# Two small attentions rebuilt with unrolled loops, and in the recurrence the corner blocks moved to ScalarE

## The reference

```python
for i in range(H):                       # L0_attn, H = 16
    q_rot, k_rot = rotary(q[:, i], freq_i), rotary(k[:, i], freq_i)
    att = einsum('btd,bsd->bts', q_rot, k_rot) * scale
    if cascade_bias is not None:
        att = att + cascade_w[i - 1] * cascade_bias
    att = softmax(causal(att))           # next head's bias comes from att
...
for t in range(T):                       # L1_attn, per sequence and head, S and R are 64 x 64
    kn = k / max(norm(k), 1e-12)
    r = clip(v - S.T @ kn, -1, 1)
    S = a * S;   S = S + b * outer(kn, v - S.T @ kn)
    R = aR * R;  R = R + g * outer(kn, r - R.T @ kn)
    o = S.T @ q + R.T @ q
...
q = lora(x, Wq, bq, Aq, Bq)              # L3_xattn, 16 heads, keys and values from the context
k, v = split(lora(feature, Wf, bf, Af, Bf))
out = lora(softmax(causal(q @ k.T / sqrt(8))) @ v, Wp, bp, Ap, Bp)
```

## Time and profile before

| | us |
|---|---|
| median of 3 runs | 3740.51 (3736.25 to 3745.74) |
| the profiled execution | 3746.5 |
| its span, first to last instruction | 3744.7 |
| l0_attn, first product to last add | 170.4 to 461.2 |
| l1_attn, first load to the next sublayer's | 1121.9 to 2421.7 |
| l3_xattn, first product to the block's end | 3414.7 to 3542.0 |
| mean granted TensorE clock (1 is 2.4 GHz) | 0.833 |

### The profile page before, as it was taken

One profiled execution on the slowest core, in us unless ns is written; L12 is line 12 of the kernel. 1 busy time (PEld: TensorE's weight loads), 2 busy tenths in 40 slices (PEclk: granted clock), 3 DMA queues, 4 the chain that ended last, 5 costly groups with the idle time before them and its releaser, 6 DMA issues. The chain is left out here.

```text
span 3744.7 us, 117402 instructions
## 1 busy us (share of the span) xinstructions
PE 2824.1 (75%) x50001; PEld 1980.9 (53%) x50009; DVE 2288.9 (61%) x5777; ACT 1433.9 (38%) x3268; POOL 606.6 (16%) x623
## 2 busy tenths in 40 slices
PE   8852347899995687878787877759998998696654
PEld 5510136444444566666666666536665665384443
DVE  3466532556546887778877887247776555564451
ACT  4312123334333343444444443426665333363220
POOL 0040032455540000000000000000000322061014
PEclk9865567899996698989988998959998998796575
DMA  2100023111101000000000000000001001251013
GB/s 81 40 0 0 0 95 111 55 37 44 43 20 44 3 4 3 4 3 4 4 4 3 4 4 4 3 10 24 24 24 42 0 0 29 71 121 44 5 35 96
DMA packets 69034, 107.01 MB, mean 29 GB/s; under 512 B 10384, under 2 KB 55072, under 8 KB 68032
## 3 DMA queue, kind: packets, MB, share of 16 engines
q1 hardware_dynamic: 56912, 78.25, 6.8%
q0 software_dynamic: 11696, 22.40, 2.4%
HBM read 87.97 MB, written 16.51 MB: 28 GB/s over the span
## 5 line engine op out<-in xcount | busy, mean ns | idle before, releaser
L2885 PE MATMUL psum<-l1d_rw,l1d_cols 64*32 64x32 f32 (+2 forms) x20480 | 246.0, 221 | 115.0 <-issue 71.2
L2394 POOL TENSOR_TENSOR l2x_qx<-l2x_q,consts 128x128 f32<-128x128 f32 x64 | 25.5, 398 | 1723.2 <-DVE l2x_q L2565 1399.5
L2885 PEld LDWEIGHTS psum<-l1d_rw,l1d_cols 64*32 64x32 f32 x20480 | 215.9, 110 | 160.8 <-issue 109.6
L2319 POOL TENSOR_SCALAR l1xs_p<-l1xs_p,l1xs_col 128x257 f32<-128x257 f32 x256 | 238.1, 932 | 243.3 <-DVE l1xs_col L2282 242.7
L2247 ACT ACTIVATE l1xs_p<-psum,l1xs_col 128x257 f32<-128x257 f32 x256 | 122.2, 477 | 256.1 <-DVE l1xs_col L2277 255.9
L2682 ACT COPY l1d_ya<-psum 128x512 f32<-128x512 f32 x160 | 94.2, 589 | 264.4 <-PE psum L2924 264.4
L2277 DVE TENSOR_REDUCE l1xs_col<-psum 128x1 f32<-128x257 f32 x256 | 107.3, 419 | 138.5 <-PE psum L2199 138.5
L3119 DVE TENSOR_TENSOR l1d_rw<-l1d_rw,l1d_tots 128x512 f32<-128x512 f32 x240 | 152.5, 685 | 26.7 <-PE psum L2885 24.9
L2199 PE MATMUL psum<-l1xs_keys,l1xs_qx 128*32 128x257 f32 x2048 | 161.8, 396 | 3.7 <-ACT l1xs_p L2247 3.7
L2211 PE MATMUL psum<-l1xs_pt,l1xs_vals 32*128 32x512 f32 x1152 | 162.0, 637 | 1.3 <-DVE l1xs_pt L2289 1.3
L2824 PE MATMUL psum<-l1d_src,l1d_wp 128*128 128x128 f32 x1024 | 144.2, 300 | 23.3 <-ACT l1d_src L2687 23.3
(11 more groups left out here) (562 smaller groups left out, 7121.1 us busy)
## 6 DMA issues: line engine op xcount, KB each, us to landing
l2f_w<-in_l2f_w SPq DMA_DIRECT2D x16, 768.0 KB, 4.7
l1xs_vals<-in_ctx_strips SPq DMA_DIRECT2D x16, 576.0 KB, 3.8
l0x_ctxT<-in_ctxT SPq DMA_DIRECT2D x16, 516.0 KB, 3.7
l1xs_keys<-in_ctxT SPq DMA_DIRECT2D x16, 516.0 KB, 3.5
l2x_ctxT<-in_ctxT SPq DMA_DIRECT2D x64, 129.0 KB, 2.1
l1d_wp<-in_l1d_wp SPq DMA_DIRECT2D x1, 2048.0 KB, 8.0
l2f_acc<-l2f_zero SPq DMA_DIRECT2D x8, 256.0 KB, 4.5
l2f_sums<-l2f_acc SPq DMA_DIRECT2D x8, 256.0 KB, 5.1
```

Source lines behind the costliest of these rows:

```text
L2319: nc.gpsimd.tensor_scalar(p[:, t % 4, :S2], p[:, t % 4, :S2], col[:, 2, t % 4:t % 4 + 1], None, ALU.mult).then_inc(s["norm"], 1)
L2885: mm = nc.tensor.matmul(k.ps[bank0 + pr + e // per * 2][b * T:b * T + T, e % per * w:(e % per + 1) * w], cols[rr, n, e * 128 + b * T:e * 1 ...
```

## The change

It rewrites `l0_attn` as one unrolled block and drops `small_scores` and `small_values`. Scores are made as in `l3_xattn`; the head loop works on two halves of 256 columns by turns, transposes go to PE with a copy on ACT, values are laid out per head (`vd`) so that a product gives the own head's rows, and the output projection is spread over the heads with widened weights (1 MB in place of 64 KB). In `l3_xattn` values and attention are multiplied per unit (one chunk and head group) with 128 rows of weights, 64 products per chunk in place of 256, and the projection out takes 16 products of 128x128 per chunk with widened weights (1 MB more to load, and 16 more products to fold the low-rank part in). In `l1_attn` ACT copies the corner blocks out of PSUM with a column of ones and zeros as scale, PE's first fill of a tile also waits for that, `turn` negates 16 elements a row in place of 1024 and needs no memset, and each part of the inversion stands one step later in DVE's order.

```diff
# l0_attn: ahead of the head loop, on PE
+            front(0)
+            pe.wait_ge(s["set"], 2)
+            for c in range(1, NCH):
+                front(c)
+                scores(c - 1)
+            scores(NCH - 1)
+            pe.wait_ge(s["vd"], NCH)
# l0_attn: the head loop
+            def turn(h, x):
+                pe.wait_ge(s["att"], h * 2 + x + 1)
+                if h < H - 1:
+                    nc.tensor.matmul(mean_ps[x][:, :half * T], k.const("meanT"),
+                                     att[:, x, h % 2].rearrange("p n s -> p (n s)"), start=True, stop=True
+                                     ).then_inc(s["mean_mm"], 1)
+                if h * 2 + x > 0:
+                    pe.wait_ge(s["t"], h * 2 + x)
+                for j in range(2):
+                    mm = nc.tensor.transpose(t_ps[:, j * 128:(j + 1) * 128], ...)
+                mm.then_inc(s["t_mm"], 1)
+            def values(h, x):
+                pe.wait_ge(s["t"], h * 2 + x + 1)
...
+                for j in range(2):
+                    for b in range(TB):
+                        n = (2 * x + j) * TB + b
+                        mm = nc.tensor.matmul(o_ps[m, n * T:(n + 1) * T], vd[:, n, h, :], attT[:, x, j, b * T:(b + 1) * T],
+                                              start=True, stop=True)
+            for h in range(H):                      # PE
+                turn(h, 0)
+                if h > 0:
+                    values(h - 1, 1)
+                turn(h, 1)
+                values(h, 0)
+                if h >= 4:
+                    out(h // 4 - 1, h % 4)
+            def first(h, x):                        # DVE
+                src = sc[:, h, half * x:half * x + half, :]
+                if h > 0:
+                    dve.wait_ge(s["mean_mm"], (h - 1) * 2 + x + 1)
+                    step(nc.vector.scalar_tensor_tensor(a[:, x].rearrange("p n s -> p (n s)"), mean_ps[x][:, :half * T],
+                                                     cw[:, h:h + 1], src.rearrange("p n s -> p (n s)"), ALU.mult, ALU.add))
...
+                step(nc.vector.tensor_reduce(mx[:, x], src, AX.X, ALU.max))
+                nc.vector.tensor_tensor(a[:, x], src, spread(mx[:, x]), ALU.subtract).then_inc(s["shift"], 1)
+            for h in range(H):                      # DVE
+                if h > 0:
+                    second(h - 1, 1)
+                second(h, 0)
+                first(h, 1)
+                if h + 1 < H:
+                    first(h + 1, 0)
# l3_xattn: values and out
-            def values(c):
...
-                for b in range(TB):
-                    r = slice(b * T, (b + 1) * T)
-                    if b > 0:
-                        pe.wait_ge(s["own_mm"], c * TB + b)
-                    for t in range(4):
-                        for h in range(4):
-                            for g in range(4):
...
+            def values(u):
...
+                for t in range(4):
+                    for h in range(4):
+                        mm = nc.tensor.matmul(o_ps[32 * h:32 * h + 32, g * 128 + t * T:g * 128 + t * T + T],
+                                              vd[:, c % 2, t, 4 * g + h, :], attT[:, u % 2, (t * 4 + h) * T:(t * 4 + h) * T + T],
+                                              start=True, stop=True)
...
+                for b in range(TB):
+                    for g in range(4):
+                        mm = nc.tensor.matmul(out_ps[:].rearrange("p (t b q) -> p b t q", t=4, b=TB)[:, b], wp[:, g, b, :],
+                                              o[:, g, :], start=g == 0, stop=g == 3)
# l1_attn
+            def keep_l(i, n):
+
+                act.wait_ge(s[("mS", "mR")[n]], i * LEVELS + LEVELS)
+                for pr in range(2):
+                    x = k.ps[2 * n + pr][:, :(384, 256)[n]].rearrange("p (h f t) -> p h f t", h=hp, t=T // 2)
+                    ins = activation(ll[:, i % 2, n, hp * pr:hp * pr + hp, :], x[:, :, n], ACT.Identity, scale=part[:, 4:5])
+                ins.then_inc(s["ll"], 1)
...
                     take_nb(i + 1)
+                if now:
+                    keep_l(i, 0)
                 if old:
                     take(i - 2, "o_mm", rd, "B", "o")
+                if now:
+                    keep_l(i, 1)
                 if mid:
                     widen(i - 1, 1)
                     widen(i - 1, 2)
...
                 if lv == 0 and i > 0:
+                    pe.wait_ge(s["ll"], i * 2)
                     pe.wait_ge(s["mR"], i * LEVELS)
...
-                        vc.copy_predicated(ll[:, i % 2, 0, hs, :], top, part_[:, :, 0, :])
...
-                        ins = vc.copy_predicated(ll[:, i % 2, 1, hs[pr], :], top, part_[:, :, 1, :])
...
-                t(vc.tensor_scalar(xi[:, :T * T], lt[:, :T * T], -1.0, None, ALU.mult))
-                t(vc.memset(xi[:, 0:T * T:T + 1], 1.0))
+                t(vc.tensor_scalar(first(xi), first(lt), -1.0, None, ALU.mult))
...
-                if mid:
-                    merge(2)
-                if now:
                     advance_s(i, 1)
                     keep_s(i, 1)
                 if mid:
-                    merge(4)
+                    merge(2)
                 if now:
                     advance_r(i, 1)
                     keep_r(i, 1)
                 if mid:
-                    merge_last(0)
+                    merge(4)
                 if now:
                     advance_s(i, 2)
                     keep_s(i, 2)
...
                 if mid:
-                    merge_last(1)
-                    turn_back(i - 1)
+                    merge_last(0)
                 if now:
                     advance_s(i, 3)
                     keep_s(i, 3)
                     advance_r(i, 3)
                     keep_r(i, 3)
+                if mid:
+                    merge_last(1)
+                    turn_back(i - 1)
+                if now:
                     keep_s(i, 4)
```

More of the change, by code:

```diff
@@ L639, in l0_attn @@
     nc, ph = k.nc, ExitStack()
-    s = {n: k.sem("l0a_" + n) for n in ("bias_mm", "shifted", "exp", "att", "turned", "kept", "steps")}
+    s = {n: k.sem("l0a_" + n) for n in ("set", "group", "p_mm", "turn", "qk", "v_mm", "vd", "ks", "sc_mm", "kept", "step", "shift", "exp",
+                                        "att", "mean_mm", "t_mm", "t", "o_mm", "o", "out_mm", "x")}
     with ph:
         wall = k.sb("l0a_w", [128, 5, D], ctx=ph)
-        wproj = k.sb("l0a_wp", [128, D], ctx=ph)
+        wp = k.sb("l0a_wp", [128, 4, 4, D], ctx=ph)
@@ new lines, in l0_attn @@
+        half = N // 256
+        a, att = k.sb("l0a_a", [128, 2, half, T], ctx=ph), k.sb("l0a_att", [128, 2, 2, half, T], ctx=ph)
+        mx, rs = k.sb("l0a_mx", [128, 2, half], ctx=ph), k.sb("l0a_rs", [128, 2, half], ctx=ph)
+        attT, o = k.sb("l0a_attT", [128, 2, 2, 128], ctx=ph), k.sb("l0a_o", [128, 2, CH], ctx=ph)
+        mean_ps, t_ps, o_ps = k.ps[4:6], k.ps[6], k.ps[7]
+        pair = lambda c, n: 4 + 2 * ((c + n) % 2)
+        block = ph.enter_context(nc.Block())
+        @block.tensor
@@ L796, in _ @@
             pe.wait_ge(s["fold"], 1)
             front(0)
+            rows(0)
             pe.wait_ge(s["set"], 3)
-            for c in range(NCH):
-                scores(c)
-                if c + 1 < NCH:
-                    front(c + 1)
-                if c > 0:
-                    values(c - 1)
+            scores(0)
+            pe.wait_ge(s["wide"], 4)
+            scores(1)
+            for g in range(4):
+                mm = nc.tensor.matmul(o_ps[:, :1], wp[:, g, 0, :], bv[:, g:g + 1], start=g == 0, stop=g == 3)
@@ L805, in _ @@
+            mm.then_inc(s["bias_mm"], 1)
+            for u in range(units):
+                c, g = u // 4, u % 4
+                if u + 2 < units:
+                    scores(u + 2)
+                if g == 0 and c + 1 < NCH:
+                    front(c + 1)
+                if u > 0:
+                    values(u - 1)
+                if g == 1 and c + 1 < NCH:
+                    rows(c + 1)
+                if g == 2 and c > 0:
                     out(c - 1)
-            values(NCH - 1)
+            values(units - 1)
@@ L807, in _ @@
             out(NCH - 1)
-        @block.gpsimd
-        def _(pool):
-            nc.gpsimd.memset(vs[:], 0.0).then_inc(s["clear"], 1)
         @block.scalar
@@ L906, in _ @@
                                   ).then_inc(s["set"], 1)
-            last = 4 * NCH - 1
-            shift(0)
-            for u in range(last + 1):
-                if u < last:
+            for g in range(4):
+                dve.wait_ge(s["wide_mm"], g + 1)
+                x = wp[:, g].rearrange("p b d -> p (b d)")
+                nc.vector.scalar_tensor_tensor(x, k.ps[(1, 2, 3, 7)[g]][:], 1.0 / 16, x, ALU.mult, ALU.add
+                                               ).then_inc(s["wide"], 1)
+            shift(0)
+            dve.wait_ge(s["bias_mm"], 1)
+            nc.vector.tensor_tensor(cols[:, 5:6], o_ps[:, :1], bcol[:, 2:3], ALU.add).then_inc(s["bias"], 1)
```

(8 more changed lines are left out.)

575 lines of the change are left out of this document (256 added, 319 removed).

## The result

The changed kernel takes 3526.4 us (median of 4 runs, 3516.4 to 3539.7) against 3743.1 before, a ratio of 0.9425 with a 95% interval of 0.9382 to 0.9467: 217 us less, where I had forecast 165. It lies in the range, between the forecast (3575) and the rival "warm and smooth" (3518). The profiled execution took 3535.4 us, 211 less than the one of before.

What follows compares the result with a forecast made beforehand. It took waits among PE, DVE and ACT to bound l0_attn, PE l3_xattn, PE and DVE l1_attn. Gains 104 + 12 + 50 = 166 from the profiled 3746.5, less 6, gave 3575 us; range 3515 to 3632.

Steps and rivals of the forecast that it cites:

- warm and smooth: Rival (c), whole kernel: gains of 122 in l0_attn, 26 in l3_xattn, 75 in l1_attn, 223 in all, 3518 us; chance 0.13.
- l0_attn, 104 forecast: The rebuilt l0_attn block falls from 290.7 to 187 us (73 front, 102 heads, 12 rest), a gain of 104 us.
- 16 x 2.40 = 38.4: l0_attn ahead of the head loop: 16 scores groups on PE at l3_xattn's price of 2.40 us, 38.4 us.
- The head loop, 102 forecast: l0_attn's 16 heads at 6.4 us, mixing about 8.0 at half clock (6.25 without projection) and 5.65 at full: 102 us.
- l3_xattn, 12 forecast: l3_xattn on PE: values 37 us less, fold and bias 9.4 and out 12 more, 3 less for waits; gain 12.
- warm end of 28: Upper end of the l3_xattn term, with PE warm: a gain of 28 us.
- l1_attn, 50 forecast: l1_attn: clip 4.35 us earlier per pass; 48 + 12 + 2 - 3 - 9 = 50 us gained.
- 48 us: l1_attn: the part of PE step y2's 56.4 us wait for DVE's clip that was to go, 48 us.
- (a): Rival, l0_attn's head loop: PE stays at 1.2 GHz, heads take 121 us, 141 us gained, 3600 us; chance 0.22.
- (d): Rival, l0_attn: the two halves don't overlap, a head takes 17.6 us, the kernel is 14 slower, 3754 us; chance 0.03.
- (b): Rival, l1_attn: PE's queue bounds it, the wait for the clip becomes issue gaps, 128 gained, 3613 us; chance 0.14.
- Weights of 1 MB more: l0_attn and l3_xattn: wider weights load during the layer norm, costed at nothing; if late, 1 or 2 us each.

Runs made afterwards that it cites:

- e6: The changed kernel with l0_attn's output projection moved ahead of the second half's mean in the head loop; 3509.9 us, ratio 0.9366 to the kernel before.
- e7: The changed kernel with each value product in l3_xattn taking 32 of its 128 rows; 3536.0 us, l3_xattn 86.9 us.
- e8: The changed kernel with l3_xattn's fold of the wide output weights placed behind the first chunk's projections; 3531.9 us, l3_xattn 88.7 us.
- e9: The changed kernel with 12 of the 16 products of l3_xattn's projection out left out; 3536.3 us, l3_xattn 83.4 us.
- e4: The kernel before with only the new order of the merges on VectorE in l1_attn; 3694.8 us, ratio 0.9851.
- e5: The kernel before with only l1_attn's corner block copies moved to ScalarE, old merge order and full negation kept; 3742.9 us, ratio 0.9996.
- e11: The changed kernel with l1_attn's sigmoid table loaded early and the second merge, merge(4), put behind the clip; 3529.3 us, l1_attn 1217.2 us.
- e3: The kernel before with the new l1_attn alone; 3704.5 us, ratio 0.9883.
- e10: The changed kernel with l1_attn's sigmoid table loaded early, in ScalarE's idle time; 3528.4 us, l1_attn 1220.7 us.

## Why the prediction was right, and where it was not

- *l0_attn, 104 forecast, 125 measured.* The term was mis-sized in its front: "16 x 2.40 = 38.4" for the scores. Twelve of the sixteen groups took 1.33 us from start to start and only the last chunk's four took 2.40; projections and value products ran mostly at the full clock too (17.5 and 5.2 us busy, taken as 21.7 and 8). The front took 57 us to the first mean, not 73 + 2, and what follows the loop 6.5, not 10. I had carried the price of a group over from a block that ran at 0.55 of the clock.
- *The head loop, 102 forecast (6.4 a head), 101 measured.* The total is right, in part by luck. The first four heads took 5.6 us on average (I had 6.25; the first, at 0.50 of the clock, took 6.28), the ten behind them 7.0 (I had a mixture of 5.65 and 8.0 that comes to 6.4), and the last head, without a mean, is short. That the granted clock parts the quick heads from the slow ones was right: with the projection, 5.54 and 6.01 us at the full clock, 7.30 at 0.73. The step that I missed is what e6 shows: the place of the projection costs 0.86 us a head by itself and brings the lower clock with it. The unseen operation, 128 rows x 32 columns, cost 0.69 / 16 = 0.043 us at full clock, near the lower end and not the 0.08 that I took.
- *l3_xattn, 12 forecast, 38 measured, past even my warm end of 28.* Two prices were wrong in the same direction: scores (29.4 us busy before, 18.9 after, taken as unchanged) and value products (7.6 busy and 3.8 waited, taken as 17). The fold was right in itself (7.0 for 8.2), but was set against a sum of PE alone. That sum was the wrong frame. Once PE is quick, VectorE's 3.65 us per scores group bound the block; in that frame the 38 us are there, since its wait for scores fell by 28.6 us (36.7 to 8.1) and that for the projection out by 11.9 (20.0 to 8.1). A chunk takes 17.4 us (3293.61 to 3311.03, VectorE's adds to X), where I had 24 to 27. PE's values, fold and scores groups hardly count there any more (e7; e8; e9, where five of the last eight groups were slow and the block no longer for it); its projection out still does (6 us in e9).
- *l1_attn, 50 forecast, 42 to 53 measured.* The mechanism was right: what stands ahead of the clip counts, and what is put off goes into VectorE's wait at level 5 (e4), though not for nothing, since its wait ahead of `advance` grew by 32 us. From y2 to y2 a pass takes 72.0 us on average (passes with all parts at work), 75.4 before; I had 71. Inside it one size was off: "48 us" of y2's wait were to go, and 32 went (56.4 to 24.4), since the gates, 14.1 us, are late next and I had not named them. What made up for it is that the fills wait less for VectorE too, 44 us before (115.0 less 71.2 of issue) and 27 after (99.4 less 72.5). y2's own time fell by 9.3 us (51.1 to 41.8; I had 12). The copies on ScalarE cost and bring nothing, as said (e5).
- *The rivals.* (a), a head loop wholly cold, and (d), halves that do not overlap, did not come: 0.78 of the clock, 6.6 us from mean to mean (92.2 us over 14 heads). The 4 us of the earlier trace rows that spoke for (a) also hold a 128x128 mask product of 0.61 us, and are not 32x32 tiles alone. (b) did not bind here; e11 suggests that it does once y2's waits are gone. (c), "warm and smooth" at 3518, was the nearest of all cases to 3526, but by luck: its l0_attn (122) is met by a warm front and not by warm heads, its l3_xattn (26) is too low and its l1_attn (75) too high.
- *Weights of 1 MB more in two sublayers* cost little, as said: ahead of l0_attn's first product PE stands idle for 1.31 us (1.84 in the earlier trace rows), ahead of l3_xattn's for 3.02 (1.32 in the earlier trace rows).

## What to carry to other kernels

In an engine's hand-written order, ask of each piece who waits behind it: moving the corner blocks to another engine gave nothing here, while existing lines put in another place gave 42 to 51 us (the merges) and 23 us (the projection out). A price measured in a block at 0.55 of the clock is not the price of the same instruction in a rebuilt block; bound it by the same row at both levels, and ask of every engine, not only of the one that binds now, what the rebuilt block would take if that engine set the pace. When a wait has been shortened, look in the new profile at which other signal arrives within half a microsecond of it before shortening it again.

## What the runs showed of the hardware that I had not expected

- Instructions on 128 rows x 32 columns that go to one group of 32 columns one behind the other take 43 ns each (16 in 0.69 us, l0_attn); those that go round four groups of columns take 14 (32 in 0.46, l3_xattn). The two stand in different blocks; no run changes the column group alone.
- The number of rows of the small value products (128 or 32) made no difference to the granted clock of the block, 0.80 and 0.81; a projection out with a quarter of its products did, 0.68.
- Two heads of l0_attn in after, with the same instructions in the same order and 7 us between them, ran at 1.00 of the clock in 5.54 us and at 0.73 in 7.30.
- l2_attn, which nothing here touches, took 276.9 us in the profiled executions of before, e3, e4, e10 and e11, and 284.5 to 284.7 in those of after, e6, e7 and e8, and 276.7 to 279.6 in the others; its granted clock was 0.96 in before and 0.93 in after. So 8 us of a whole kernel's time can come and go in one untouched sublayer, which is why single stages were compared here, and several profiles of the same stage where they scatter.
